# Scatters of edge counts into a count matrix: writing the count, or adding it to the cleared cell

## The reference, cut to what matters

```python
x = _layernorm(x + _L0_gnn_ref(x, src, dst, L0_gnn_W, L0_gnn_b))              # softmax over the edges of a node
x = _layernorm(x + _L1_gnn_ref(x, edge_index, edge_attr_4, ...))              # messages of edges, summed at dst
x = _layernorm(x + _L2_gnn_ref(x, edge_index, Wl1, bl1, Wr1, Wl2, bl2, Wr2))  # two mean aggregations
x = _layernorm(x + _L3_gnn_ref(x, edge_index, W1l, b1, W1r, W2l, b2, W2r))    # two more
# each aggregation of the last two layers:
summed = jax.ops.segment_sum(h[src], dst, num_segments=num_nodes)
agg = summed / jnp.maximum(deg, 1.0)[:, None]
h = agg @ Wl.T + bl + h @ Wr.T
```

## Time and profile before

| | us |
|---|---|
| median of 2 runs | 4443.63 (4442.38 to 4444.88) |
| time of the profiled execution | 4448.21 |
| its span, first to last instruction | 4446.5 |
| SOFT pass | about 84 to 1100 |
| MESSAGE pass, POOL's gathers and scatters | 1262 to 2767 |
| late scatters on POOL | 2846 to 3352 |
| convolutions 1 to 3 on PE | 3435 to 4441 |

### The profile page before, as it was taken

How to read it: one execution, slowest core, us unless ns; L and a number is a source line. 1 busy time by engine, 2 the same in 40 slices (tenths; PEclk the granted TensorE clock), 3 DMA queues, 4 the chain that set the end, 5 groups by cost and what they waited for, 6 DMA issues and landing times.

```text
span 4446.5 us, 61952 instructions
## 1 busy us (share of the span) xinstructions
PE 3142.0 (71%) x18737; PEld 2339.7 (53%) x18737; DVE 2669.0 (60%) x5868; ACT 1571.3 (35%) x3684; POOL 2506.6 (56%) x2587
## 2 busy tenths in 40 slices
PE   1666666664766655666666666396667999999999
PEld 0444444443644444544445454274445777788777
DVE  5999999998656666666666665810004444333333
ACT  2888888886333333333333333200001111111000
POOL 7777777776667777777777777777771000000000
PEclk9999999999997777777777776697788999999999
DMA  6666666665144545444545543263444666766776
GB/s 209 227 231 232 230 228 229 228 227 171 55 122 129 130 134 134 131 132 129 136 129 131 134 133 99 77 220 121 138 145 150 253 244 236 261 252 237 282 277 219
DMA packets 387597, 797.89 MB, mean 179 GB/s; under 512 B 207412, under 2 KB 264600, under 8 KB 361128
## 3 DMA queue, kind: packets, MB, share of 16 engines
q1 hardware_dynamic: 182882, 567.06, 37.4%
q0 software_dynamic: 82320, 90.28, 9.3%
q10 hardware_dynamic: 122166, 137.91, 8.8%
HBM read 581.03 MB, written 213.92 MB: 179 GB/s over the span
## 4 chain that ended last, share of the span: by engine, by line
POOL 34%; PE 22%; issue 12%; DMA 2%; DVE 2%; ACT 0%; DVEq 0%; POOLq 0%; ACTq 0%
PE ps L1189 20%; POOL area L778 17%; POOL adj L789 8%; POOL adj L865 8%; POOL area L844 1%; PE ps L1072 1%; DMA adj<-out_ring 1%; DMA area<-sums,end_row 0%; DMA area<-src_table,early 0%; PE ps L1064 0%; DMA area<-adj 0%; PE ps L1119 0%; DVE out_ring L1891 0%; DMA adj<-copies_ring,cell_ring 0%; DVE out_ring L1893 0%
## 5 line engine op out<-in xcount | busy, mean ns | idle before, releaser
L778 POOL DMA_INDIRECT area<-src_table,early x784 | 755.2, 963 | 240.7 <-issue 240.4
L778 POOL DMA_INDIRECT area<-relu_table,early x784 | 741.5, 946 | 239.1 <-issue 233.0
L949 PE MATMUL ps<-ident,area 128*96 128x128 f32 x1568 | 432.2, 371 | 518.1 <-DMA area<-src_table,early 517.6
L949 PEld LDWEIGHTS ps<-ident,area 128*96 128x96 f32 x1568 | 312.5, 233 | 691.2 <-DMA area<-src_table,early 661.8
L1189 PE MATMUL ps<-second,area 128*128 128x288 bf16 x5194 | 652.9, 287 | 0.2 <-DVE second L1835 0.2
L1189 PEld LDWEIGHTS ps<-second,area 128*128 128x128 f16 x5194 | 509.3, 98 | 129.0 <-DVE second L1835 0.5
L1662 DVE SCALAR_TENSOR_TENSOR second<-second,area,ps 128x512 bf16<-128x512 f32 x784 | 537.7, 739 | 0.0
L961 PE MATMUL ps<-ident,area 96*128 96x96 f32 x2352 | 417.5, 343 | 133.0 <-ACT out_ring L1254 128.1
L961 PEld LDWEIGHTS ps<-ident,area 96*128 96x128 f32 x2352 | 350.7, 206 | 225.2 <-DVE area L1723 205.6
L1694 DVE TENSOR_TENSOR_SCAN area<-flags,area,ps 96x512 f32<-96x512 int8 x196 | 250.0, 1276 | 349.7 <-ACT dump L1242 346.1
L789 POOL DMA_INDIRECT adj<-copies_ring,cell_ring x392 | 389.6, 994 | 119.5 <-issue 118.6
(11 more groups left out here) (330 smaller groups left out, 4997.0 us busy)
## 6 DMA issues: line engine op xcount, KB each, us to landing
area<-adj SPq DMA_DIRECT2D x147, 1632.0 KB
area<-adj SPq DMA_DIRECT2D x55, 1568.0 KB
adj<-early SPq DMA_DIRECT2D x102, 816.0 KB
soft_sums<-out_ring ACTq DMA_DIRECT2D x196, 384.0 KB
second<-key_dram SPq DMA_DIRECT2D x98, 512.0 KB, 5.0
sums<-out_ring ACTq DMA_DIRECT2D x196, 192.0 KB
second<-caps_dram SPq DMA_DIRECT2D x98, 192.0 KB, 4.2
area<-dst_table SPq DMA_DIRECT2D x392, 48.0 KB
```

The source lines that it names most:

```text
L778: pool.indirect_dma_start(out=src_rows[:, s, c, :], out_offset=None, in_=gather_table[p], in_offset=bass.IndirectOffsetOnAxis(ap=src_cols[ ...
L949: nc.tensor.matmul(ps[0:F, s % 2, at], src_rows[:, s, c, :], ident[:, :], start=False, stop=False)
```

## The change

Two scatters get one more argument, by which a DMA adds the value to what stands in the cell and does not overwrite it. The third scatter, that of the joints at L821, stays as it is. No instruction is added, removed or moved on any engine, and no wait changes; the lists of cells, the counts and the clearing are the same. Since the cells that are read are cleared and get one count each, the sum is the count.

```diff
                     pool.indirect_dma_start(
                         out=adj_all, out_offset=bass.IndirectOffsetOnAxis(ap=cell_ring[:, s, c:c + 1], axis=0),
-                        in_=copies_ring[:, s, c:c + 1], in_offset=None).then_inc(adj_made[s], 16)
+                        in_=copies_ring[:, s, c:c + 1], in_offset=None, compute_op=ALU.add).then_inc(adj_made[s], 16)
...
                             pool.indirect_dma_start(
                                 out=adj_all, out_offset=bass.IndirectOffsetOnAxis(ap=cell_late[:, c:c + 1], axis=0),
-                                in_=copies_late[:, c:c + 1], in_offset=None).then_inc(late_made[i % 2], 16)
+                                in_=copies_late[:, c:c + 1], in_offset=None, compute_op=ALU.add).then_inc(late_made[i % 2], 16)
```

## The result

The changed kernel takes 4922.18 us (median of 2 runs, 4918.32 to 4926.04) against 4443.63 us: a ratio of 1.1075, 95% interval 1.1049 to 1.1102. It is **slower by 478.5 us**, and the longer POOL instruction that the prediction named is where the time went. The profiled execution has a span of 4924.3 us, 477.8 us more than before.

A forecast was written before the change was run, and what follows sets the result against it. POOL's instructions were taken to bound the MESSAGE pass and the late stage: 176 + 176 = 352 us on the profiled 4448.2 gave 4800, less 4.6 for the median, 4795 us. The range was 4435 to 5210 us.

The forecast's parts named there:

- the mechanism given 0.47: L789 and L865: POOL's instruction gets longer by between 114 and 983 ns; time 4795 us, own range 4535 to 5210.
- What bounds the kernel: MESSAGE pass and late stage: POOL alone paces both, so each ns on one of 782 scatters is a ns of the program.
- POOL's instruction: L789 and L865: each adding scatter takes 0.45 us more, 176 us in the MESSAGE pass and 176 us in the late stage.
- the middle between nothing and 0.98 us: Price of an adding scatter on POOL: 0.45 us, between no growth and a second instruction's worth of work, 983 ns.
- the 460 ns of L764: Gathers at L764: 21 had a mean of 1434 ns against 974 for the other 28; taken as nearest to 0.45 us.
- +769 us: Both scatters: upper end if the reading core sets the length and all of the instruction's time doubles.
- No change: Rival, chance 0.33: reads of the cells hide beside POOL's 0.97 us, growth stays under 114 ns; 4444 us.
- Landings cost nothing: Both stages: additions land later, but slack of 23 and 31 us (MESSAGE pass) and 14 us (late batches) covers it.
- DMA engines: Late stage: an addition takes 0.22 us on each engine of the 1.27 us between issues, so it costs nothing.
- The rival of a queue that takes additions one by one: Both stages: case of the DMA queue as the bound (chance 0.17); 17.6 us a scatter, 16,400 us in all.
- The other scatter, L821: Scatter of the joints, not edited: a sign of the longer instruction was that it stays at 971 ns.

## Why the prediction was right, and where its size was off

**The time.** 4922 us lies in the range of 4435 to 5210, but that range took in both no change and an instruction twice as long, so that alone says little. What counts is that the mechanism given 0.47 is the one that came; its middle, 4795, was 127 us too low. The pass grew by 251 us and not by 176, and the late stage took 729 us and not 680.

**What bounds the kernel: right.** Each ns on a scatter came back as a ns of the program: 475.9 us of POOL's own lengthening against 477.8 of span. That the two agree to 2 us is partly chance: the pass began 5.5 us later, and the pauses before L865 shrank by 4.1 us. (4 x 1.27 + 2 x 1.30 is 7.68, not 7.67; nothing hangs on it.)

**POOL's instruction: right in kind, too small in size.** The term was 782 x 0.45 = 352 us; it measured 248.5 + 227.4 = 475.9, or 0.61 us a scatter. The step that was off is the choice of the middle between nothing and 0.98 us, with the 460 ns of L764 as its support. That figure was misread: it is a mean over a few outliers, as the line's own view shows (min/median/max ns).

```profile
L764 POOL DMA_INDIRECT out_ring<-node_rows_dram,early x21: 943/948/5570, 11.9 to 47.1; - x21
```

Two of the 21 took 5.57 and 4.18 us, which is 7.9 of the 10.2 us that the 21 took above their median, and that median, 948 ns, is that of any gather. So the support falls away; what is left is the middle of two bounds, and that it came as near as 0.45 to 0.61 is luck. The reason given for the middle, more entries on the reading side, is a third of the truth at most: some 420 of 593 ns come with the instruction whatever the list holds, and a gather, whose second read needs no list, pays the same. The prediction took a rule from the Trainium skill ("Collectives: The Full Stack", The bandwidth ceiling: an add takes two read descriptors where a copy takes one) as doubling the whole instruction, +769 us, which was not reached. For the part that goes by the entry the trace agrees with two in place of one, 2.6 ns against 1.2. But a plain instruction here goes by the entry only for 971 - 837 = 134 ns between 16 and 128 entries, so this is the smaller part.

**No change: out.** Its condition was a growth of less than 114 ns; even two lone additions grew by over 600.

**Landings cost nothing: right.** DVE's wait for them went from 144.4 to 266.8 us, in windows of 1400 and 1650 us, and POOL's idle time before L789 stayed at 119.6 us. The waits for batches in the late stage fell from 1.5 to 0.3 us, where a batch now has 8 x 1.87 = 15 us in place of 10. The last landing is 2.7 us later.

**DMA engines: right that they don't bind, the term too small.** 0.22 us on each engine was forecast for a scatter, 0.37 measured, of a pitch of 1.87. The rival of a queue that takes additions one by one at 2.2 us each, 17.6 us a list, is out: a lone list of 8 entries an engine landed in 3.1 us. The prediction drew from the Trainium skill ("DMA: Bandwidth & Descriptors", Two DMAs through the same engine are not ordered) that additions overlap; those 3.1 us agree with it but don't show it, since 8 one after another at 0.37 / 8 = 0.05 us each would land as soon.

**The other scatter, L821: wrong by a little.** It was to stay at 971 ns and took 1115 and 990 behind the adding scatters:

```profile
L821 POOL DMA_INDIRECT adj<-one_h,joint_cell x2: 990/1052/1115, 3022.4 to 3023.8; - x2
```

In the run where only the MESSAGE pass adds it took 987 and 1254, and there the second is the longer one; where only the late stage adds, behind plain scatters, 958 and 961. Additions between gathers are also longer, 1630 ns against 1564 in a row of their own kind, and the last scatters of the pass, which have no gathers between them, take 1.55 to 1.56 us. It looks as if a change of kind costs something; that wasn't tried, and two instances a run don't show it.

**Open:** what POOL does in the 420 ns. The runs show that it comes with each adding instruction, even with a single row for each engine, alone or in a row; they don't show what it is. Nor was any operation but the addition tried, so whether the price is the addition's or that of any such operation stays open.

## What to carry to other kernels

Here an indirect DMA that adds occupied POOL for 0.6 us more than one that writes a list of 128 (0.44 us more for 16), so where POOL sets the pace and the target is cleared and hit once, write. Where an addition is needed, use full lists: most of its price, as of the plain instruction's, is paid per instruction. To price an option that the trace doesn't show, changing one or two instances, like the two joints here, tells its duration and moves the time by next to nothing (4440.80 against 4439.66 us). And look at the median and the longest of a group before a mean is used as a price, as with L764 here; and before a wait in the chain is believed, look at when that which it waited for was done.

## What had not been expected of the hardware

- An adding list of n entries has n - 16 packets more than a plain one: 112 for 128 entries in all four kinds tried, 48 for 64, 16 for 32, none for 16.
- Of a plain list's 971 ns only about 1.2 ns an entry goes by the length of the list (837 ns with 16 entries), so an instruction with an eighth of the entries is 14% shorter.
- The clock granted to PE in the late stage was 0.83 before and 0.74 after, where PE was busy for 359 of 506 us and then for 383 of 729. Nothing was lost by it, since POOL, with its work and pauses, fills the stage's length both times:

```profile
2846.00:3352.00 506.00, 359.33 (x2491) 269.45 (x2491) 80.39 (x179) 13.89 (x29) 382.95 (x390) 0.83 0.46 156
```

```profile
3101.00:3830.00 729.00, 382.87 (x2500) 278.85 (x2501) 79.63 (x179) 13.89 (x29) 609.85 (x390) 0.74 0.50 108
```

The rows are of a view by stretches: the stretch, its length, then busy us and instructions of PE, weight loads, DVE, ACT and POOL, the granted clock, the DMA share and GB/s; the first is of before, the second of after. The two levels are 1.2 and 2.4 GHz, so 0.83 and 0.74 are means over time at either.
